# Cross-attention and routed experts on one core: layer norm, turning and gate products of finished batches placed in the attention, late expert weights issued by SyncE

## What is computed

```python
x = x + xattn(layernorm(x), ctx)      # 8 batches of 256 queries, 1601 keys, 256 features, 16 heads
x = x + ffn(layernorm(x))             # 2048 tokens

# ffn
base_y = silu_mul(x @ base_gate_up) @ base_down            # shared expert, inner width 512
probs = softmax(xf @ gate_w)                               # 8 experts
w, idx = top_k(probs, 2); w = w / w.sum(-1)
for e in range(8):
    out = out + comb[:, e:e+1] * (silu_mul(xf @ expert_gate_up[e]) @ expert_down[e])
return out + base_y
```

## Time and profile before

| what | us |
|---|---|
| median of 3 runs | 1318.78 |
| lowest and highest | 1318.33, 1321.24 |
| the profiled execution | 1325.05 |
| its span, first to last instruction | 1323.3 |
| attention, to the barrier | 0 to 972.5 |
| statistics, normalising, gate | 972.5 to 998.6 |
| shared expert | 998.6 to 1074.5 |
| first turning of a slot tile | 1087.1 |

### The profile page before, as it was taken

One profiled execution on the slowest core, in us unless ns is written; L12 is line 12 of the kernel. 1 busy time (PEld: TensorE's weight loads), 2 busy tenths in 40 slices (PEclk: granted clock), 3 DMA queues, 4 the chain that ended last, 5 costly groups with the idle time before them and its releaser, 6 DMA issues. The chain is left out here.

```text
span 1323.3 us, 23152 instructions
## 1 busy us (share of the span) xinstructions
PE 1217.8 (92%) x8526; PEld 913.5 (69%) x8526; DVE 786.3 (59%) x1648; ACT 686.1 (52%) x952; POOL 362.1 (27%) x266
## 2 busy tenths in 40 slices
PE   4689999999999999999999999999959946999995
PEld 4667777777777777777777777655527845888884
DVE  4256767677667666767766677778456422444442
ACT  3337666666666656666666666556623211222221
POOL 3311113322323422322322223112014720323222
PEclk9889999999999999999999999999979977999998
DMA  4656476578767677776576775574155359333333
GB/s 137 210 171 143 132 177 163 161 204 221 219 194 209 188 192 219 234 208 194 168 191 214 203 199 150 167 189 130 45 222 235 123 195 375 57 52 53 53 52 86
DMA packets 160734, 222.85 MB, mean 168 GB/s; under 512 B 65312, under 2 KB 132264, under 8 KB 160560
## 3 DMA queue, kind: packets, MB, share of 16 engines
q1 hardware_dynamic: 148768, 194.14, 51.1%
q0 software_dynamic: 8656, 14.63, 5.5%
q10 hardware_dynamic: 3200, 12.58, 2.4%
HBM read 129.63 MB, written 93.58 MB: 169 GB/s over the span
## 5 line engine op out<-in xcount | busy, mean ns | idle before, releaser
L616 DVE TENSOR_REDUCE mx<-side 128x1 f32<-128x400 f32 (+1 forms) x1024 | 534.6, 570 | 139.3 <-PE side L468 130.3
L511 ACT ACTIVATE prob<-st 128x1024 f32<-128x1024 f32 (+1 forms) x416 | 411.8, 1022 | 185.8 <-PE st L489 184.7
L468 PE MATMUL side<-kst,qst 96*128 96x400 f32 (+1 forms) x1024 | 329.4, 382 | 3.6 <-DVE mx L616 2.4
L489 PE MATMUL st<-qst,kst 97*128 97x512 f32 (+1 forms) x832 | 266.2, 403 | 7.1 <-DMA qst<-mrow 3.6
L468 PEld LDWEIGHTS side<-kst,qst 96*128 96x128 f32 x1024 | 189.7, 189 | 114.0 <-issue 37.4
L501 PE MATMUL acc<-prob,v 128*32 128x256 f32 (+1 forms) x3328 | 206.8, 384 | 0.0
L489 PEld LDWEIGHTS st<-qst,kst 97*128 97x128 f32 (+1 forms) x832 | 147.9, 186 | 21.3 <-ACT prob L511 8.9
L648 POOL TENSOR_TENSOR clo<-raw,chi 128x768 fp32r<-128x768 f32 (+1 forms) x32 | 60.9, 1904 | 366.5 <-ACT chi L542 366.5
L501 PEld LDWEIGHTS acc<-prob,v 128*32 128x32 f32 (+1 forms) x3328 | 95.4, 110 | 79.5 <-issue 22.8
L654 POOL TENSOR_TENSOR flo<-fc,fhi 128x768 fp32r<-128x768 f32 (+1 forms) x32 | 61.0, 1905 | 214.6 <-ACT fhi L555 214.6
L1378 POOL DMA_INDIRECT token_sums<-yg,xg x39 | 60.9, 1562 | 182.4 <-DVE yg L1540 157.1
(11 more groups left out here) (187 smaller groups left out, 1650.2 us busy)
## 6 DMA issues: line engine op xcount, KB each, us to landing
kst<-parts_at SPq DMA_DIRECT2D x90, 400.2 KB, 5.9
parts_at<-parts SPq DMA_DIRECT2D x48, 384.0 KB, 6.5
w_at<-piece_hi SPq DMA_DIRECT2D x27, 512.0 KB, 6.6
w_at<-piece SPq DMA_DIRECT2D x27, 512.0 KB, 5.8
v<-v_at SPq DMA_DIRECT2D x32, 408.0 KB
wall<-w_at SPq DMA_DIRECT2D x8, 1536.0 KB, 19.9
wall<-w_at ACTq DMA_DIRECT2D x8, 1536.0 KB, 18.4
raw<-ctx_t SPq DMA_DIRECT2D x24, 384.0 KB, 5.4
```

The costliest lines, as they stand in the source:

```text
L468: pe.matmul(side[u.bank][:, 0:w], t.qst[0:96, pair, col * P:(col + 1) * P], t.kst[0:96, pair, o:o + w], start=True, stop=True).then_inc(si ...
L489: mm = pe.matmul(into[0:rows, i * 2 * NQ:(i + 1) * 2 * NQ], t.kst[0:97, GP * g + i, s * P:s * P + rows], t.qst[0:97, GP * g + i, :], start ...
L511: act.activation(prob[0:rows, s, :], st[(KT * g + s) % 2][0:rows, :], ACT.Exp, scale=float(DH) ** -0.5).then_inc(exp_done, 1)
L616: dve.tensor_reduce(mx[:, hq, r:r + 1], side[u.bank][:, 0:RANGES[r][1]], AX.X, ALU.max)\
```

## The change

- **Finished batches.** In the first group's phase of the next batch VectorE takes statistics of `res` (behind `out`), GpSimd raises to -0.5, VectorE normalises into `xn` in step 11 (`0 norm`), and SyncE stores that as `rows_at`. In phases 28 to 31 (`EXTRA`), batches 0 to 6 are loaded back one by one (`again`), turned by TensorE (`rows`), copied twice by ScalarE (`xh`, `xt`), and GpSimd takes the low part; in steps 5 to 11 of phase 31 their gate products are made. The last batch goes this way in the FFN, between the first `gate_up`s.
- **Shared expert's weights.** Pieces start at phase 0, and SyncE loads `wb` at the end of phases 29 and 30. Buffers of the attention that are free by then lend the room (`sp_lent_free`).
- **FFN.** TensorE starts with `gate_up(0, 0)` with no load to wait for. GpSimd has two chunks (`POOL_TC` = 2), with the sum of the first ahead of the second product of the second; `counts` stands behind `down(0)`. `EARLY` is 3, and experts lie in `wall` in reverse. SyncE issues the weights of experts 3 to 7, two loads each, with one tile's rows between two experts.

```diff
+LAST = PHASES - GROUPS
+EXTRA = {(LAST, 8): ("rows", 0), (LAST + 1, 5): ("rows", 1), (LAST + 1, 8): ("rows", 2), (LAST + 2, 5): ("rows", 3),
+         (LAST + 2, 8): ("rows", 4), (LAST + 3, 2): ("rows", 5), (LAST + 3, 4): ("rows", 6)}
+EXTRA.update({(LAST + 3, 5 + i): ("gate", i) for i in range(B - 1)})
...
+        def pe_turn_rows(pe, u, b):
+            pe.wait_ge(again_in, 16 * (b + 1))
+            bank_free(pe, u)
...
+        def act_turned_rows(act, u, b):
+            unit_full(act, u)
+            after(act, rows_lo, b)
+            turned = side[u.bank][:, :].rearrange("p (c n) -> p c n", c=KC)
+            act.activation(k.xh[:, :, b * NQ:(b + 1) * NQ], turned, ACT.Copy)
+            act.activation(k.xt[:, :, :], turned, ACT.Copy).then_inc(side_free[u.bank], 1)
...
+        def dve_statistics(dve, b):
+
+            dve.wait_ge(x1_ready, GROUPS * (b + 1))
+            for q in range(QT):
+                dve.bn_stats(t.stats[:, q, :], res[:, q, :]).then_inc(ln_done, 1)
+            dve.wait_ge(ln_done, 5 * b + QT)
+            for q in range(QT):
+                dve.bn_aggr(k.mv[:, QT * b + q, :], t.stats[:, q, :]).then_inc(ln_done, 1)
...
+        def dve_normalise_rows(dve, b, u_turn):
+
+            dve.wait_ge(ln_rstd, b + 1)
...
+        def sp_load_rows(sp, b, u_last):
+            if u_last is not None:
+                unit_full(sp, u_last)
+            sp.wait_ge(rows_out, 16 * (b + 1))
+            sp.dma_start(k.again[:, :, :], rows_at[:, QT * b:QT * (b + 1), :]).then_inc(again_in, 16)
...
+                        for _, done in rows_of_phase(p):
+                            sp_load_rows(sp, done, rows_unit(done - 1) if done > 0 else None)
...
                         if last + 1 < PHASES:
                             sp_max_row(sp, body_unit(b, at, g, "tm", 0), behind(b, g, 1)[1])
+                        if g == 0 and at > 0:
+                            sp_store_rows(sp, b - 1)
+                        if LAST < p <= LAST + 2:
+                            sp_load_shared(sp, p - LAST - 1)
...
-POOL_TC = 1
+POOL_TC = 2
...
-EARLY = 4
+EARLY = 3
...
-WEIGHTS_FROM = 3
+WEIGHTS_FROM = 0
...
-                load_expert(sp, wall[:, (EARLY - 1) * W2:EARLY * W2], EARLY - 1, early_in)
                 store_y(TC - 1)
-                for n in range(XG, SLOT_TILES):
+                sp.wait_ge(y_out, 16 * TC)
+                for e in range(EARLY, E):
+                    for a in range(2):
+                        load_part(sp, place(e), w_at, e, a, late_in)
+                    load_rows(XG + e - EARLY)
+                for n in range(XG + E - EARLY, SLOT_TILES):
                     load_rows(n)
...
-                act.wait_ge(y_out, 16 * TC)
-                for e in range(EARLY, E):
-                    load_expert(act, wall[:, e * W2:(e + 1) * W2], e, late_in)
...
+                between = {(0, 1): last_rows, (0, 2): last_gate, (0, 3): turn_gate, (1, 0): counts}
```

More of the change, by code:

```diff
@@ L664, in pool_residual @@
             after(pool, x1_out, 16 * b)
+            after(pool, rows_done, QT * b)
             unit_out(pool, u_resid)
@@ L1118, in weight_piece, with gate_products, load_part, ffn @@
     return (E, p) if p < PIECES else divmod(p - PIECES, PIECES)
-def ffn(nc, ident, x1, w_at, slot_x, acc, gate_w, out):
+def gate_products(pe, k, bank, b):
+    i = 0
+    for c in range(KC):
+        for w, a in ((k.gwh, k.xh), (k.gwl, k.xh), (k.gwh, k.xl)):
+            mm = pe.matmul(bank[0:E, 0:NQ], w[:, c, :], a[:, c, b * NQ:(b + 1) * NQ], start=(i == 0),
+                           stop=(i == 3 * KC - 1))
+            i += 1
+    return mm
+def load_part(eng, dst, w_at, e, a, s):
+    eng.dma_start(dst[:, a * WE:(a + 1) * WE].rearrange("p (i n) -> p i n", n=PIECE).bitcast(F32),
+                  w_at[e, a].rearrange("i p n -> p i n")).then_inc(s, 16)
+def ffn(nc, ident, both, x1, rows_at, w_at, slot_x, acc, out):
     with ExitStack() as ctx:
@@ L1589, in copy_y, with last_rows, last_gate, gate_exponential @@
                         act.activation(y_copy[q % 2], py[q % 2][:, 0:D], ACT.Copy).then_inc(y_copied, 1)
+                def last_rows():
+                    act.wait_ge(turned, 1)
+                    act.activation(xh[:, :, last], turn, ACT.Copy).then_inc(xh_done, 1)
+                def last_gate():
+                    act.wait_ge(logit_full, 1)
+                    act.activation(lt[:, last], py[2][0:E, 0:NQ], ACT.Copy).then_inc(lt_done, 1)
+                def gate_exponential():
+                    act.wait_ge(sub_done, 1)
+                    act.activation(ex[:, :, :], ex[:, :, :], ACT.Exp).then_inc(gate_exp, 1)
+                between = {(0, 1): last_rows, (0, 2): last_gate, (0, 3): gate_exponential}
                 for c in range(TC):
@@ L1665, in _, with last_rows, last_gate @@
-                mm.then_inc(lt_turned, 1)
+                def last_rows():
+                    pe.wait_ge(n_done, QT)
+                    for q in range(QT):
+                        for c in range(KC):
+                            mm = pe.transpose(turn[:, c, q * P:(q + 1) * P], rows[:, T - QT + q, c * P:(c + 1) * P],
+                                              ident[:, :])
+                    mm.then_inc(turned, 1)
+                def last_gate():
+                    pe.wait_ge(xl_done, 1)
+                    gate_products(pe, both, py[2], B - 1).then_inc(logit_full, 1)
@@ L1708, in _ @@
                             down(c - 1)
-                    if c == 0:
-                        counts()
+                        if (c, f) in between:
+                            between[c, f]()
                 down(TC - 1)
```

439 lines of the change are left out of this document (238 added, 201 removed).

## The result

| kernel | median us | lowest, highest | profiled execution |
|---|---|---|---|
| before | 1318.55 | 1318.25, 1321.24 | 1325.05, span 1323.3 |
| changed | 1330.28 | 1328.78, 1333.77 | 1333.77, span 1332.0 |

A forecast was written before the change was run, and what follows sets the result against it. TensorE was taken to bound the attention, chains of waits the stretches behind it. 1325.05 + 20.1 + 0.8 - 12.7 - 12.6 + 6.2 = 1326.9, times 0.9953 = 1320.6, say 1320 us; range 1306 to 1332.

The forecast's parts named there:

- the sum: Whole kernel: all parts added to the profiled time and scaled, about 1320 us, chance 50%.
- signs of being wrong: Attention's end (T0) moves under 10 us, scatters start under 50 after it, or tiles wait over 12.
- Part 1: Attention, batches 0 to 5: statistics and normalising on VectorE delay TensorE, +6 us.
- Part 2: Attention phases 28 to 30: statistics, turning of finished batches' rows and ScalarE's copies hold banks, +5 us.
- Part 3: Attention phase 31: wait for rows behind shared weights, another unit of rows and gate units, +8.5 us.
- Part 4: Attention's end to first scatter: time saved on normalising goes into GpSimd's second chunk; scatter at T0 + 53.2, +1 us.
- Part 5: Scatters and first tiles: no weights awaited for tile 0, ScalarE free for tile 1, -25 us.
- Part 6: Slot tiles: late weights on SyncE's queue make rows of tiles 6 to 9 late, +6 us.
- starved tiles: Slot tiles: adds take 8 us or more while weights stream, rows late; 18 instead of 6, 1332 us, chance 14%.
- attention rival: Attention: bank delays are caught up in TensorE's later waits, 8 us instead of 20, 1309 us, chance 28%.

The follow-up runs named there:

- e1: Changed kernel with one tile's rows behind each half of a late expert instead of each whole one: 1336.18 us, 1.012 of the kernel before.
- e7: Changed kernel with rows behind each half expert, finished batches' loads ahead, and statistics and normalising moved later, together: 1319.40 us, 1.000 of the kernel before.
- e3: Changed kernel with VectorE's statistics behind step 8's score maxima and normalising in step 10: 1321.21 us, 1.001 of the kernel before.
- e6: Changed kernel with one chunk of the shared expert on GpSimd instead of two: 1348.18 us, 1.012 of the kernel before.
- the spread kernel: Changed kernel with statistics and normalising moved, finished batches' loads ahead, and late experts spread over the tiles: 1313.01 us, 0.988 of the kernel before.

## Why the prediction was partly right

The likeliest single case, at 50%, was the sum, 1320 with 1314 to 1326; of the three outcomes slower had 0.40, faster 0.38 and no change 0.22. Measured are 1330, 0.8% slower: outside the range of the sum, and inside the whole one (1306 to 1332) near its end. None of its signs of being wrong came (T0 moved by 24, the first scatter stood at 51.9, the tiles waited 9.1). But that it stayed inside is partly luck: parts 2 and 6 were 9.6 too low together, the others 4.7 too high.

- **Part 1, statistics: right in mechanism and size.** 0.95 per phase in theory; 0.9 to 1.0 measured, 5.5 in all with what other phases gain or lose, for 6.3. That the place was the cause, and not the instructions, is shown by moving them.
- **Part 2, phases 28 to 30: the transfer that was left out.** 1.6, 1.65 and 1.65 were predicted; 1.5, 6.3 and 1.3 measured, and 1.5, 1.8 and 1.5 once the loads stood ahead. The step that failed is the sentence in part 1 that SyncE's wait for the normalised rows stands some 20 us before its users: the user I looked at was the next phase's scores. Behind that wait (1.6) stood keys, queries and values, 5.5 us of issues, and behind those the new load that TensorE wants in step 5 of the same phase, which then took 7.9 to land. It came 2.3 late, and 6.8 us at half clock about doubled that.
- **Part 3, phase 31: right.** A wait of 3.5 was predicted, 3.25 measured, 7.8 for 8.9 in all. Turning the order of the two loads round took 5 of it away.
- **Part 4: right, and for the reason given.** 53.2 against 51.9: the time that normalising gave up went into GpSimd's second chunk. The run with one chunk scattered 14 earlier.
- **Part 5: right.** -15.1 where -12.7 was predicted, since the scatters took 45.0 instead of 46.9 and the first rows 2.2 instead of 2.6; -11.7 for -12.6. (The first product of tile 2 stood at 1113.1 in the timeline of the kernel before, so the 26.2 was 26.0; and the prediction's own terms put tile 0's turning at T0 + 102.7, not 102.)
- **Part 6: mechanism right, term mis-sized.** 6.2 predicted, 11.6 measured. The waits came at tiles 7 to 9, as forecast, but as 2.95, 2.14 and 4.04 instead of 1.1, 2.3 and 2.8. An add under load landed 8.0 to 8.2 after its issue, as predicted; but the prediction had taken the 0.7 to the next add off the 8.9 and never put it back, so SyncE sent the rows of tiles 6 to 9 8.8 to 8.9 apart where its landings are 8, 7.5 and 8 apart. And the rows that were waited for landed 3.8 to 4.6 after their issue, with a new expert right behind them. The rest, 2.5, is the clock, which I had left out: 0.50 for 3.4 us behind two of the three waits. The rival "starved tiles", 18 at a chance of 14%, had this mechanism; the time came out between the two.

The attention rival (its cost absorbed) is refuted: TensorE's phases grew by the whole delay. The profiled pair differs by 8.7 where 1.9 was forecast; the 6.8 between are +1.9 (start, not the change's), -0.8 (part 1), +4.2 (part 2), -1.1 (part 3), -1.3 (part 4), -1.5 (part 5) and +5.4 (part 6). The medians lie 3 us further apart than the profiled executions, because the profiled one of the kernel before was 6.5 over its median and that of the changed kernel 3.5.

## What to carry to other kernels

A new DMA on an in-order queue must be costed at the place where its data is first wanted, behind everything that the queue waits for and issues ahead of it; two small reorderings of that kind were worth 10 us here. Small work on a nearly full engine cost nearly its whole length ahead of a rotating buffer's reader and at most 0.1 a phase a few steps later, in a gap that existed already. When a chain of small transfers runs beside large ones, count how many of the small ones run while a large one moves, and not the bytes: cutting the large ones into halves made it worse.

## What was not expected of the hardware

- An indirect add of 128 rows takes 4.5 us from one to the next alone, 7.2 to 9.8 with 1.5 MB issued just ahead (e1 and e7), and 8.1 to 10.4 with 3.1 MB (most of them 8.7 to 9.1, the longest in e3 and e6), though 3.1 MB take 7.8 at 401 GB/s. What sets the excess of 2.7 to 5.9 us, if not the bytes, was not tried.
- On chips B and C TensorE stood in the shared expert, while GpSimd scattered, with nothing shown as awaited, in the kernel before's order of loads too; 12.5 us at the longest, in the spread kernel:

```profile
1073.66 2.07 PE L1797 MATMUL py<-wb,hh 128*128 128x256 f32 x8 [12.55 <-issue]
```

In the profiles of chip A there is none, nor in the first pair. The medians of the kernel before are 1319.6 on A, 1337.5 and 1331.2 on B and C. The cause is open; no run here takes the scatters away from beside the products.
